# Transposes moved to later slots beside the attention scores of a gated Flamingo block on one core

## The reference

```python
x = x + tanh(g_xattn) * attention(layernorm(x), ctx)      # self + cross, then @ Wp + bp
h = layernorm(x)
logits = h @ router_w + router_bias; probs = softmax(logits); top_w, top_i = top_k(probs, 2)
routed = sum_e combine[:, e] * (silu(h @ gate_w[e]) * (h @ up_w[e])) @ down_w[e]   # expert 15: identity
shared = (silu(causal_conv(h)) * (h @ shared_up_w)) @ shared_down_w
x = x + tanh(g_ffn) * (shared + routed)
```

## Time and profile before

| | us |
|---|---|
| three runs | 1543.89, 1546.71, 1549.03 |
| median | 1546.71 |
| the profiled execution | 1540.59 |
| its span, first to last instruction | 1538.5 |
| TensorE busy in the span | 1426.7 (93%) |
| VectorE busy | 1145.7 (74%) |
| ScalarE busy | 896.0 (58%) |
| GpSimd busy | 901.9 (59%) |

### The profile page before, as it was taken

The page is one execution under the profiler, slowest core; times in us unless marked ns, Lnnn a source line. Parts: engine busy times, 40 slices in busy tenths (PEclk is TensorE's granted clock), DMA queues, the critical chain, the costliest instruction groups (busy, mean ns, idle before and its releaser), DMA issues.

```text
span 1538.5 us, 36199 instructions
## 1 busy us (share of the span) xinstructions
PE 1426.7 (93%) x11288; PEld 948.6 (62%) x11288; DVE 1145.7 (74%) x3026; ACT 896.0 (58%) x1907; POOL 901.9 (59%) x1643
## 2 busy tenths in 40 slices
PE   4899999999999999999999999999979989898997
PEld 3556556655566566555655665665546778787675
DVE  6777887878778887878788787878644555565686
ACT  3466676666667676666667666665723555565210
POOL 4245566664756666575756657475654555665782
PEclk8899999999999999999999999999999999999999
DMA  6745454545454554645464454545555565454794
GB/s 169 198 131 138 140 151 141 172 135 165 135 160 146 157 169 120 183 133 151 134 177 144 136 180 126 159 134 172 178 152 160 169 221 170 150 153 143 230 351 165
DMA packets 184123, 250.01 MB, mean 162 GB/s; under 512 B 32024, under 2 KB 134560, under 8 KB 183936
## 3 DMA queue, kind: packets, MB, share of 16 engines
q1 hardware_dynamic: 149680, 185.60, 42.0%
q0 software_dynamic: 13008, 36.65, 6.6%
q10 hardware_dynamic: 21248, 25.46, 5.0%
HBM read 150.06 MB, written 95.97 MB: 160 GB/s over the span
## 4 chain that ended last, share of the span: by engine, by line
PE 63%; DVE 18%; ACT 11%; issue 5%; DMA 2%; POOL 1%; SPq 0%; DVEq 0%; ACTq 0%; POOLq 0%
PE vector_bank L2025 8%; PE pv_self L1529 8%; DVE nmax L1288 7%; PE scalar_bank L1465 7%; PE vector_bank L1502 5%; PE vector_bank L1575 4%; PE vector_bank L1439 3%; PE vector_bank L1499 3%; ACT q L857 3%; PE scalar_bank L1452 2%; PE scalar_bank L1455 2%; PE scalar_bank L1453 2%; ACT parts L866 2%; PE scalar_bank L2012 2%; ACT parts L873 2%
## 5 line engine op out<-in xcount | busy, mean ns | idle before, releaser
L1288 DVE TENSOR_REDUCE nmax<-vector_bank 128x1 f32<-128x384 f32 (+4 forms) x832 | 511.2, 639 | 74.4 <-PE vector_bank L1502 70.0
L929 ACT ACTIVATE pt<-scalar_bank 128x512 f32<-128x512 f32 x640 | 362.7, 605 | 175.6 <-PE scalar_bank L1465 167.1
L746 POOL TENSOR_SCALAR_AFFINE_SELECT pt<-pt 128x256 f32<-128x256 f32 (+1 forms) x640 | 222.7, 362 | 206.4 <-ACT pt L929 184.4
L1465 PE MATMUL scalar_bank<-stack 99*64 99x512 bf16 (+4 forms) x1280 | 284.2, 319 | 2.3 <-ACT pt L929 1.0
L1502 PE MATMUL vector_bank<-stack 96*128 96x128 bf16 (+3 forms) x1024 | 244.0, 301 | 0.0
L1854 POOL DMA_INDIRECT rows<-pt x143 | 139.1, 973 | 117.3 <-DVE pt L1983 63.2
L1499 PE MATMUL vector_bank<-tri,ident_b 128*128 128x128 bf16 (+2 forms) x704 | 175.3, 249 | 21.5 <-DMA stack<-qk_scratch 10.5
L1529 PE MATMUL pv_self<-pt,vst 128*32 128x512 f32 (+3 forms) x2048 | 161.1, 438 | 0.1
L705 POOL DMA_INDIRECT rows<-xn,slot x128 | 132.8, 1037 | 44.2 <-issue 26.3
L1499 PEld LDWEIGHTS vector_bank<-tri,ident_b 128*128 128x128 bf16 x704 | 67.0, 97 | 145.2 <-DVE nmax L1288 59.9
L2025 PE MATMUL vector_bank<-pt 128*128 128x128 f32 x1144 | 151.2, 275 | 0.1
(11 more groups left out here) (320 smaller groups left out, 2858.9 us busy)
## 6 DMA issues: line engine op xcount, KB each, us to landing
qk_scratch<-parts SPq DMA_DIRECT2D x31, 1200.0 KB, 4.5
stack<-qk_scratch SPq DMA_DIRECT2D x120, 192.0 KB, 3.0
pt<-rows SPq DMA_DIRECT2D x143, 132.0 KB
stack<-qk_scratch SPq DMA_DIRECT2D x248, 72.0 KB, 2.5
stack<-qk_scratch SPq DMA_DIRECT2D x124, 128.0 KB, 3.0
stack<-qk_scratch SPq DMA_DIRECT2D x240, 36.0 KB, 2.1
pt<-rows SPq DMA_DIRECT2D x8, 1024.0 KB, 8.7
stack<-rows SPq DMA_DIRECT2D x8, 1024.0 KB, 11.5
```

What stands on the lines that cost most here:

```text
L746: pool.affine_select(out=v, in_=v, compare_op=ALU.is_ge, fill=0.0, base=0, pattern=pat, channel_multiplier=-1).then_inc(masked, 1)
L929: act.activation(dst, bank(kind, b, ("st", c, k))[:, :], ACT.Exp, scale=SCALE).then_inc(scalar_drained, 1)
L1288: dve.tensor_reduce(dst, src, axis=AX, op=ALU.max, negate=True).then_inc(vector_drained, 1)
L1465: return pe.matmul(out, stack[c][0:rows, head, key0:key0 + nk], stack[c][0:rows, head, q0:q0 + nq], start=True, stop=True, **kw)
```

## The change

Numbers in the tables change, nothing else. The result's transposes go from slots 1 and 2 to 2 and 3 of half 0, the output products from 4 to 7 to 5 to 8, and the row statistics with them. The maxima's transposes go from slots (0, 2), (0, 16), (1, 2) and (1, 16) to (0, 4), (0, 20), (1, 4) and (1, 19). The next rows' transposes go from (1, 13) and (1, 15) to (1, 14) and (1, 16). The line in `FIRST_UNITS` is that of the prologue, where no other unit stands between.

```diff
-PREV_UNITS = {(0, 1): ("yT", 0), (0, 2): ("yT", 1), (0, 4): ("wp", 0), (0, 5): ("wp", 1), (0, 6): ("wp", 2), (0, 7): ("wp", 3),
+PREV_UNITS = {(0, 2): ("yT", 0), (0, 3): ("yT", 1), (0, 5): ("wp", 0), (0, 6): ("wp", 1), (0, 7): ("wp", 2), (0, 8): ("wp", 3),
...
-             (0, 2): ("mT", 0, 1), (0, 16): ("mT", 1, 0), (1, 2): ("mT", 1, 1)}
+             (0, 4): ("mT", 0, 1), (0, 20): ("mT", 1, 0), (1, 4): ("mT", 1, 1)}
```

More of the change, by code:

```diff
@@ L71, in occupant @@
         return kind, b, self.names(kind)[at]
-PREV_UNITS = {(0, 1): ("yT", 0), (0, 2): ("yT", 1), (0, 4): ("wp", 0), (0, 5): ("wp", 1), (0, 6): ("wp", 2), (0, 7): ("wp", 3),
+PREV_UNITS = {(0, 2): ("yT", 0), (0, 3): ("yT", 1), (0, 5): ("wp", 0), (0, 6): ("wp", 1), (0, 7): ("wp", 2), (0, 8): ("wp", 3),
               (0, 17): ("rT", 0), (0, 18): ("rT", 1), (0, 19): ("rT", 2), (0, 20): ("rT", 3), (0, 21): ("rl",), (0, 22): ("rm",), (1, 12): ("rk",)}
-ROUTE_STEPS = {(0, 5): ("stats", 0), (0, 6): ("stats", 1), (0, 7): ("stats", 2), (0, 8): ("stats", 3), (0, 10): "aggregate", (0, 14): "normalise", (0, 23): "max", (1, 0): "shift", (1, 2): "sum",
+ROUTE_STEPS = {(0, 6): ("stats", 0), (0, 7): ("stats", 1), (0, 8): ("stats", 2), (0, 9): ("stats", 3), (0, 10): "aggregate", (0, 14): "normalise", (0, 23): "max", (1, 0): "shift", (1, 2): "sum",
                (1, 3): "invert", (1, 4): "probs", (1, 5): "top", (1, 6): "index", (1, 7): "as float",
@@ L88 @@
 CUR_UNITS = {(1, 6): ("tU", 0, 1, "x"), (1, 11): ("tU", 0, 1, "s"),
-             (0, 2): ("mT", 0, 1), (0, 16): ("mT", 1, 0), (1, 2): ("mT", 1, 1)}
-NEXT_UNITS = {(1, 8): ("v", 0), (1, 9): ("v", 1), (1, 10): ("vc",), (1, 13): ("xT", 0), (1, 15): ("xT", 1), (1, 16): ("mT", 0, 0)}
+             (0, 4): ("mT", 0, 1), (0, 20): ("mT", 1, 0), (1, 4): ("mT", 1, 1)}
+NEXT_UNITS = {(1, 8): ("v", 0), (1, 9): ("v", 1), (1, 10): ("vc",), (1, 14): ("xT", 0), (1, 16): ("xT", 1), (1, 19): ("mT", 0, 0)}
 LN_ROWS = {(1, 7): 0, (1, 9): 1, (1, 11): 2, (1, 12): 3}
@@ L147, in attention_phase @@
     BESIDE = [spread(5), spread(6)]
-    FIRST_UNITS = {(1, 0): [("sm", 0, u) for u in range(SM_PRE, NSM // 2)] + [("v", 0), ("v", 1), ("vc",)], (1, 13): [("xT", 0)], (1, 15): [("xT", 1)],
+    FIRST_UNITS = {(1, 0): [("sm", 0, u) for u in range(SM_PRE, NSM // 2)] + [("v", 0), ("v", 1), ("vc",)], (1, 14): [("xT", 0)], (1, 16): [("xT", 1)],
                    (1, 1): [("sm", 0, u) for u in range(NSM // 2, NSM // 2 + 1)] + [("mT", 0, 0)],
```

## The result

The changed kernel is slower: 1555.92 us median of 15 runs (1549.68 to 1563.08), against 1542.5 us for the kernel before in the same series. The ratio is 1.0098, with a 95% interval of 1.0074 to 1.0122, so some 15 us more (13.4 between the medians) where I had forecast 2. Its profiled execution took 1558.88 us.

A forecast was written before the change was run, and what follows sets the result against it. The sixteen-sequence loop was taken to bound the kernel, ScalarE or VectorE pacing stretches. Loss 0.23 less gain 0.09 gives 0.14 us a sequence, 2.1 us over 15; forecast median 1548.5 us, own range 1544 to 1553, overall 1540 to 1556.

The forecast's parts named there:

- the third stretch: Slots (1, 2) to (1, 12): TensorE 0.67 us ahead, less a 0.13 us copy, so 0.54 us reach the routing ranks.
- Slots (0, 2) to (0, 9): Result transposes and output products in half 0: copies later by 0.20 us against 0.21 us of scores, nothing won or lost.
- Slots (0, 16) to (0, 22): Maxima transpose leaves slot 16 of half 0: gain 0.09 us a sequence, at worst a loss of 0.23.
- Slots (1, 13) to (1, 20): End of half 1: second transpose of next rows falls behind attention products; loss 0.23 us a sequence, the 0.54 included.
- DMAs: Maxima transposes' DMAs on SP's queue start later but cost nothing; slot 12 scores waiting for one would disprove it.
- Rival 1: Faster: the 0.54 us is kept, the next rows' low part not delaying the maxima; 1537.2 us, chance 0.20.
- Rival 2: Slower: an exponential gets ahead of ScalarE's copy of the second transpose, loss there 0.70 us; 1555.9 us, chance 0.23.
- Rival 3: No change, since ScalarE or VectorE paces each stretch: 1546.7 us; chance 0.57 together with the forecast.
- The page that the prediction set aside: Rule that VectorE's next operation waits for an empty pipeline: low part, cast and reduction 0.18 us longer, time 1551.5 us.

The follow-up runs named there:

- experiment 5: Kernel before with VectorE's router steps from probabilities to weights one slot later in half 1: ratio 1.0091, middle sequence 68.60 us.
- 8: Kernel before with GpSimd's half 1 subtraction cut to 32 columns and maxima transpose (1, 1) in slot 4: 1531.96 us, single execution; middle sequence 67.33 us.
- experiment 1: Kernel before with only the transpose of maxima (1, 1) moved, slot 2 to slot 4 of half 1: ratio 0.9997, middle sequence 67.87 us.
- 7: Kernel before with GpSimd's half 1 subtraction of the third part cut to 32 columns: 1539.63 us, single execution; middle sequence 67.79 us.
- experiment 3: Kernel before with only the change's first slots of half 0 (result transposes, output products, statistics, maxima (0, 1)): ratio 1.0027, middle sequence 68.11 us.
- experiment 4: Kernel before with only the transpose of maxima (1, 0) moved, slot 16 to slot 20 of half 0: ratio 0.9994, middle sequence 67.85 us.
- experiment 2: Kernel before with only the change's end of half 1 (next rows' transposes slots 14, 16; maxima (0, 0) slot 19): ratio 1.0089, middle sequence 68.70 us.
- experiment 11: As experiment 2, but the second transpose of the next rows in slot 15, ahead of the attention products: 1548.44 us, single execution; middle sequence 68.03 us.
- experiment 12: Kernel before with maxima transposes (1, 0) in slot 20, (1, 1) in slot 4, and GpSimd's half 1 subtraction in two pieces: 1535.13 us, ratio 0.9948.
- 6: Kernel before with router steps one slot later and the transpose of maxima (1, 1) in slot 4 of half 1: ratio 1.003, middle sequence 68.32 us.

## Why the prediction was wrong

- *The step that failed* is the end of the third stretch: "From there VectorE works almost without a gap up to the routing ranks at 515.25, so 0.54 us arrive there." I read that VectorE had no gap, and took each of its lengths as fixed. The gap was in a length: L1160 lasted 0.49 us where 0.21 is its own time (experiments 5 and 8), and its end hung on GpSimd. Of the 0.54 us 0.07 arrived (experiment 1); with GpSimd's subtraction cut away, 0.45 (8 against 7). 0.47 us by 15 sequences are 7 us of the miss.
- *Slots (0, 2) to (0, 9)*: mis-sized. I had 0, it is 0.17 us (experiment 3), 2.6 us in all. The second copy came where I had it (ScalarE an activation later), but the products began at 12.91 and not at 12.82, because they start 0.14 us behind the end of the copy and not 0.07. And I took their length as fixed: they take 0.10 us more, with their first weights no longer loaded ahead of the wait.
- *Slots (0, 16) to (0, 22)*: right, -0.08 us (experiment 4) for -0.09. The next maxima do claim their bank, with a wait of 0.29 us that was not there before.
- *Slots (1, 13) to (1, 20)*: right, and it is the larger part of the loss; only its price against the 0.54 was wrong. I had 0.77 us there (0.23 net with the 0.54), experiment 2 measured 0.77, with the half microsecond of idle VectorE and the wait in slot 19. The path is as described: over the attention products, the second transpose, ScalarE's copy and the low part (experiment 11).
- *DMAs*: right for the middle sequences, where no score unit waits for one. The last of those of the second transpose land 17.4 us into the sequence; the scores of slot 12 start at 19.5. Outside them it was wrong. In round `first` of the changed kernel the scores of the same shape do wait, 1.33 us, which I had named as the sign against this part, and two score units behind the middle sequences wait 0.37 and 0.39 us; in the kernel before no matmul waits for one of these DMAs. I had read one middle sequence only. What this costs is not separated from the scatter of those rounds.

```profile
72.89 0.62 PE L1465 MATMUL scalar_bank<-stack 99*64 99x512 bf16 x4 [1.33 <-DMA stack<-mT]
```

- *Rival 1* (the gain is kept) failed on the same step, and on its own condition: the low part would have had to start by 518.65 on the clock of the kernel before, and started at 519.73. *Rival 2* named nearly the time, 1555.9, but by luck. No exponential got in front of ScalarE's copy, and its figure starts from a median of 1546.7 where the fifteen runs of the kernel before have 1542.5; as a ratio it is 1.006 and not 1.0098. *Rival 3* (no change) is outside the interval.
- *The page that the prediction set aside*: the section "The DRAIN you can't avoid" of the Trainium skill's "VectorE: DVE Perf Modes" says itself that a next operation that is not held starts earlier. So the rows did not contradict it, and the reductions of the changed kernel start each 0.60 us as well (three in 1.88).

With -0.07 in place of -0.54 and 0.17 in place of 0, my sum is 0.78 us a sequence, against 0.80 measured, 12 us in all. The measured 15 (11 to 19 by the interval) hold this. The other 3 stay open, but the record has a lead. The slow kernels of experiments 2 and 5 too measure more by their ratios (13.8 and 14.0 us) than 15 times their middle sequences give (11.5 and 10.0), and the mean granted clock of their runs is 0.987 and 0.986 where the kernel before has 0.989 in the same series.

The Trainium skill, "SBUF — State Buffer", section "Who interferes with whom", has the rule that would have told me: a VectorE instruction with two inputs in SBUF contends with a GpSimd instruction that reads SBUF, whoever issues first has the shared ports for its whole instruction and the other is blocked, while a reduction never contends. The traces agree for L1160, 0.21 against 0.49 and 1.05 us, and for the reductions, 0.69 either way. L1063 has only one tensor as input, so this rule does not name it; the section counts its operation, `tensor_scalar`, among those that can enter a mode that uses both ports and then contend. No trace here shows the mode. They show 0.40 us against 0.91.

## What to carry to other kernels

Before you carry a gain along an engine's list, compare each instruction's duration with the shortest one of the same shape elsewhere in the trace: a longer one can be a wait without a row, and its end may not move. The opposite holds too: an instruction that is at its own length now can be held when it is moved (experiment 5). A gain in front of such an instruction was worth almost nothing here; cutting the operation that held it in two, so that the first piece ended where the other engine arrived, freed it. And when a transfer between engines (transpose, copy, low part) is moved, see what long block it is moved behind: here one slot of one transpose was 0.67 us a sequence.

## What the runs showed of the hardware

- The hold is per instruction: between two GpSimd instructions that stand directly behind each other, VectorE gets its turn (0.57 us with pieces of 0.94, 0.21 with a cut where it arrives).
- It is decided by a tenth of a microsecond or so. By the starts in the trace L1063 came 0.03 us ahead of GpSimd's addition and was held for 0.5 us all the same; 0.17 ahead, it was not, and the addition took 0.82 us in place of 0.73. So starts as close as 0.03 us do not tell who came first.
- TensorE's clock fell to about half for some 3.6 us in single sequences, each time at the output products. Three windows of the kernel before, one ahead of the fall, one in it and one at the same place of the sequence before:

```profile
740.20:743.60 3.40, 2.25 (x14) 1.03 (x13) 2.25 (x6) 3.40 (x9) 1.59 (x6) 1.00 0.11 40
743.65:745.50 1.85, 1.85 (x6) 1.22 (x5) 0.69 (x1) 0.63 (x2) 1.54 (x2) 0.53 0.24 80
...
674.10:680.00 5.90, 5.33 (x30) 3.86 (x29) 4.01 (x9) 3.94 (x8) 4.57 (x7) 1.00 0.18 59
```

The granted clock is 0.53 there, near the 1.2 GHz level, and such a sequence is 1.67 us longer. Just before it TensorE was busy in 2.25 of 3.40 us, with waits of 0.55, 0.26 and 0.31 us, but it had nearly the same waits in the sequence before, where the clock did not fall. The kernel before has one such sequence in its trace, that of experiment 12 five, which are 8 us of its profiled execution (five by 1.67). The changed kernel and experiments 3, 6 and 7 have none. It is a part of the scatter of the runs; what brings it on stays open.
